# Strided 512-byte block loads for an fp32 conditional MLP kernel: every fourth unit in a tile, one transfer for two W slices, and a reordered expert turn

## The chip, the core and the metric

The kernel runs on one core of a Trainium2 chip. The metric is device time in microseconds of one execution: 1680.95 us for the kernel before, the median of 3 runs (1678.97 to 1681.01).

## What is computed

```python
# x (64, 128, 512) fp32; cat_ids (64,) in 0..63; exp_ids (64,) in 0..15
x = x + (einsum('bsd,bdh->bsh', x, W[cat_ids]) + b[cat_ids][:, None, :])            # L0, W (64, 512, 512)
h = gelu(einsum('bnd,hd->bnh', x, fc1_w) + fc1_b)                                     # fc1_w (2048, 512), exact gelu
shared = einsum('bnh,sh->bns', h, fc2_w) + fc2_b                                      # fc2_w (384, 2048)
expert = einsum('bnh,bph->bnp', h, experts_w[exp_ids]) + experts_b[exp_ids][:, None, :]  # experts_w (16, 128, 2048)
x = x + concat([shared, expert], -1)
```

Each of the 64 batches picks its own L0 matrix (1 MB) and its own expert (1 MB).

## The kernel before, in words

**Tiling.** 16 groups of GB = 4 batches. The 2048 hidden units are cut into NC = 16 tiles of 128, one per step c. In step c TensorE does `fc1(g, c)` (12 matmuls of 128x512: 4 slices of D, each as three fp32r products of high and low parts), `fc2(g, c-1)` (12 matmuls, 3 for each of 4 batches; 384 shared columns and 128 of the expert) and, in the eight steps of `L0_STEPS`, two slices (6 matmuls) of the L0 product of the next group. All weights and activations are split into a high part (ACT casts) and a low part (VectorE subtracts, all at the helper's L599).

**Layouts.** TensorE contracts over the partitions, so x, y (the result of L0), h and the experts must be transposed. The shared weights and the first group's x and y are transposed by TensorE (`turn`, L745), in the first group only. In all later groups it is done by DMA and VectorE: a DMA brings 32x32 blocks to their place (x: L341, y by way of a DRAM copy: L524, experts: L386), where each contiguous piece in DRAM is r = 32 floats, 128 bytes, and `nc.vector.transpose` turns all blocks of a 128x512 tile (x L614, y L627, experts L643). Hidden tile c of the kernel is rows `hidden_rows(c)*128 ...` of fc1_w; a quad of four steps shares one load of expert blocks (`load_experts`, 4 batches x 4 DMAs of 64 KB).

**Order.** Every engine runs an order written out by hand. VectorE in step c: low parts of W slices (`w_low`) and of x (`x_low`) if the step has L0 slices, `copy_last` (L661), `e_low`, at c = 0 the four results of the previous group (L680), then `turn_next_e` (the turn of expert tile c+1, L643) before `h_high` (L668) and `h_low` for c > 0 (after `h_low` for c = 0), then `turn_x` at c = 0 and at the end of a batch's L0 slices, `turn_y` two steps after them, `y_sum` (L634); after step 15 four `y_low`. In the first group `prep_low` of one shared weight tile stands between `h_high` and `h_low` and one at the end of the step. ACT: `w_high`, `x_high`, `e_high`, y DMAs, gelu (L544), `prep_high` with the next prep DMA. SP issues all other DMAs in order: in `load_l0_in(g+1, c)` first x blocks, then W slices (two 256 KB transfers into two slots, `w_in[0]`, `w_in[1]`, each behind the `w_lo` of its slot's last user), then the L0 bias and x; then at c = 0 the stores of the previous group, then the expert blocks of batch (c+1)%4. GpSimd adds biases (L463, L473, L474).

**Who waits for whom.** `fc2(g, c)` waits for `h_lo`, `e_lo` and `last_ready` of tile c; an L0 slice waits for `w_lo` and `x_lo`; `fc1(g+1, 0)` waits for all four `y_lo`. `turn_e` of a quad's first tile waits for 16 DMAs.

Of the kernel before, what the change touches and what calls it, by code (L numbers as in the profile page):

```python
# [25 lines left out]
ACT = mybir.ActivationFunctionType  # L26
P = 128
# [3 lines left out]
def build(nc, x, cat_ids, exp_ids, l0_w, l0_b, fc1_w, fc1_b, fc2_w, fc2_b, exp_w, exp_b, out):  # L31
# [17 lines left out]
    L0_STEPS = (1, 3, 5, 7, 9, 10, 11, 12)  # L49
# [5 lines left out]
    with ctx:  # L55
# [41 lines left out]
        b1_rows = x_raw[0:NC, 0:P]  # L97
# [20 lines left out]
        w_in = [sem(f"w_in{i}") for i in range(WSLOTS)]  # L118
# [17 lines left out]
        b1_turned = sem("b1_turned")  # L136
# [8 lines left out]
        b1_ready = sem("b1_ready")  # L145
# [79 lines left out]
        def hidden_rows(c):  # L225

            return (c % QUAD) * (NC // QUAD) + c // QUAD
# [81 lines left out]
        def load_prep(eng, t):  # L309
# [3 lines left out]
            dst = prep_tile(t) if PREP[t][0] == "fc1" else prep_tile(t).rearrange("p (k h) -> p k h", k=QUAD)  # L313
            eng.dma_start(dst, prep_src(t)).then_inc(prep_in[prep_slot(t)], 16)
# [3 lines left out]
        def _(sp):  # L318
# [12 lines left out]
            def load_x_blocks(G, b):  # L331
# [12 lines left out]
            def load_w(G, j, cat):  # L344

                if first(G):
                    after(sp, w_lo, j - W0SLOTS + 1)
                else:
                    after(sp, w_lo, G * NC + j - WSLOTS + 1)
                k = j % KD  # L350
                sp.dma_start(w_slot(G, j), l0_w[bass.ds(cat, 1), k * P:(k + 1) * P, :].rearrange("o d n -> (o d) n"))\  # L351
                  .then_inc(w0_in[j % W0SLOTS] if first(G) else w_in[j % WSLOTS], 16)
# [516 lines left out]
```

## Time and profile before

| | us |
|---|---|
| time, median of 3 runs | 1680.95 (1678.97 to 1681.01) |
| the profiled execution's own time | 1681.4 |
| its span, first to last instruction | 1679.6 |
| TensorE busy / VectorE busy / ACT busy / GpSimd busy | 1639.4 / 1176.4 / 551.9 / 195.1 |
| mean granted TensorE clock | 0.997 |

A granted clock of 1.00 is the 2.4 GHz level, 0.5 the 1.2 GHz level. Matmuls are pipelined, so the time that one costs is read from the distance between starts of blocks, not from its own duration. The idle time in brackets in a row is the engine's idle time before the row, with what released it. SPq and ACTq are the issuing of DMAs.

### The profile page before, as it was taken

The page shows a single profiled execution, that of the slowest core. Times are in us where ns is not written, and L with a number is a line of the kernel's source. Part 1 is how long each engine was busy: PE and PEld are TensorE (multiplying, and loading weights), DVE is VectorE, ACT ScalarE, POOL GpSimd, SP SyncE. Part 2 cuts the span into 40 slices and gives each one's busy share as a digit, 9 for nine tenths or more (in the row PEclk, how much of TensorE's full clock was granted, in tenths as well). Part 3 has the DMA queues.
Part 4 walks back from the last instruction along what each step waited for, and adds up shares of the span by engine and source line. Part 5 has one row for each costly group of instructions (what it writes and reads, how often), then busy time and mean ns, then how long its engine had stood idle before and what let it go on. Part 6 is the DMA issues. An engine that isn't in the chain of part 4 may idle for free.

```text
span 1679.6 us, 28015 instructions
## 1 busy us (share of the span) xinstructions
PE 1639.4 (98%) x7065; PEld 1315.8 (78%) x7065; DVE 1176.4 (70%) x2004; ACT 551.9 (33%) x927; POOL 195.1 (12%) x195
## 2 busy tenths in 40 slices
PE   7899999999999999999999999999999999999999
PEld 5778887877878778787877878778787787878887
DVE  5677667776777767776776677767777677767754
ACT  4343333333323333333332333333333333333321
POOL 0200100111020010200102001110200102001110
PEclk9999999999999999999999999999999999999999
DMA  7886776757677575775767767686775757757630
GB/s 207 185 190 150 147 149 147 156 129 162 127 163 151 131 156 118 167 159 133 149 133 160 156 144 157 131 157 135 163 153 131 155 118 164 163 131 151 134 61 26
DMA packets 884826, 243.44 MB, mean 145 GB/s; under 512 B 803688, under 2 KB 818168, under 8 KB 884732
## 3 DMA queue, kind: packets, MB, share of 16 engines
q1 hardware_dynamic: 740732, 203.75, 57.1%
q10 hardware_dynamic: 144000, 38.82, 10.7%
q14 instruction: 82, 0.67, 0.1%
q8 instruction: 12, 0.20, 0.1%
HBM read 209.93 MB, written 32.51 MB: 144 GB/s over the span
## 4 chain that ended last, share of the span: by engine, by line
PE 66%; SPq 20%; issue 8%; DMA 3%; DVE 2%; ACT 1%; DVEq 0%
PE ps_out L814 30%; PE ps_h L799 14%; PE ps_e L799 13%; PE ps_y L786 8%; SPq L386 8%; SPq L341 4%; SPq L320 2%; DMA e_blocks<-in_L_cond_experts_w 2%; SPq L399 2%; SPq L351 1%; SPq L393 1%; PE ps_t L745 1%; DVE e_whole L643 1%; DVE h L599 1%; DVE w2e L599 1%
## 5 line engine op out<-in xcount | busy, mean ns | idle before, releaser
L814 PE MATMUL ps_out<-w2e,h 128*128 128x512 f32 x3072 | 758.0, 396 | 10.0 <-DVE h L599 10.0
L814 PEld LDWEIGHTS ps_out<-w2e,h 128*128 128x128 f32 x3072 | 574.3, 188 | 152.5 <-DVE h L599 15.9
L799 PE MATMUL ps_e<-y_t,w 128*128 128x512 f32 x1536 | 376.8, 395 | 1.4 <-DVE y_t L599 1.4
L799 PE MATMUL ps_h<-y_t,w 128*128 128x512 f32 x1536 | 375.7, 394 | 0.0
L799 PEld LDWEIGHTS ps_e<-y_t,w 128*128 128x128 f32 x1536 | 290.7, 189 | 66.9 <-DVE y_t L599 1.6
L799 PEld LDWEIGHTS ps_h<-y_t,w 128*128 128x128 f32 x1536 | 288.5, 188 | 65.7
L643 DVE STREAM_TRANSPOSE e_whole<-e_blocks 128x512 f32<-128x512 f32 x256 | 182.0, 711 | 109.3 <-DMA e_blocks<-in_L_cond_experts_w 100.9
L530 ACT CAST w2e<-e_whole 128x512 fp32r<-128x512 f32 x256 | 158.6, 620 | 284.4 <-PE ps_out L814 157.4
L463 POOL TENSOR_TENSOR x_raw<-x_raw,b_all 128x512 f32<-128x512 f32 x60 | 85.3, 1422 | 1354.9 <-DMA x_raw<-in_x 1303.2
L499 ACT CAST w_split<-w_raw 128x512 fp32r<-128x512 f32 x244 | 145.7, 619 | 243.7 <-DMA w_raw<-in_L_cond_W 174.4
L599 DVE TENSOR_TENSOR w_split<-w_raw,w_split 128x512 fp32r<-128x512 f32 x244 | 161.1, 688 | 84.6 <-ACT w_split L499 83.7
L668 DVE CAST h<-g_raw 128x512 fp32r<-128x512 f32 x256 | 120.8, 472 | 125.4 <-ACT g_raw L544 124.0
L786 PE MATMUL ps_y<-w_split,x_t 128*128 128x512 f32 x732 | 193.1, 399 | 12.0 <-DVE x_t L599 9.6
L544 ACT ACTIVATE g_raw<-ps_e,b 128x512 f32<-128x512 f32 x128 | 88.1, 688 | 344.9 <-PE ps_e L799 302.3
L599 DVE TENSOR_TENSOR w2e<-e_whole,w2e 128x512 fp32r<-128x512 f32 x256 | 191.7, 749 | 9.9 <-ACT w2e L530 9.8
L599 DVE TENSOR_TENSOR h<-g_raw,h 128x512 fp32r<-128x512 f32 x256 | 192.7, 753 | 8.4
L786 PEld LDWEIGHTS ps_y<-w_split,x_t 128*128 128x128 f32 x732 | 137.2, 190 | 49.9 <-DVE w_split L599 14.8
L544 ACT ACTIVATE g_raw<-ps_h,b 128x512 f32<-128x512 f32 x128 | 87.8, 686 | 198.9 <-PE ps_h L799 188.8
L661 DVE CAST w2e<-w2e 128x512 fp32r<-128x512 f32 x256 | 115.2, 450 | 25.6 <-PE ps_out L814 25.4
L473 POOL TENSOR_TENSOR resid<-y,b_all 128x384 f32<-128x384 f32 x64 | 73.3, 1145 | 49.4 <-DMA out<-resid 49.1
L627 DVE STREAM_TRANSPOSE w_raw<-x_blocks 128x512 f32<-128x512 f32 x30 | 21.3, 711 | 67.7 <-DMA x_blocks<-y_rows 67.7
L614 DVE STREAM_TRANSPOSE x_whole_t<-x_blocks 128x512 f32<-128x512 f32 x60 | 41.9, 699 | 15.7 <-DMA x_blocks<-in_x 15.6
(71 smaller groups left out, 431.3 us busy)
## 6 DMA issues: line engine op xcount, KB each, us to landing
e_blocks<-in_L_cond_experts_w SPq DMA_DIRECT2D x1024, 64.0 KB, 2.9
w_raw<-in_L_cond_W SPq DMA_DIRECT2D x248, 256.0 KB, 2.9
out<-resid SPq DMA_DIRECT2D x64, 256.0 KB, 4.7
x_blocks<-in_x SPq DMA_DIRECT2D x240, 64.0 KB, 2.4
b_all<-in_L_cond_b SPq DMA_DIRECT2D x60, 256.0 KB, 4.3
x_raw<-in_x SPq DMA_DIRECT2D x60, 256.0 KB, 4.6
y_rows<-y ACTq DMA_DIRECT2D x60, 256.0 KB, 2.8
x_blocks<-y_rows ACTq DMA_DIRECT2D x240, 64.0 KB, 3.7
```

The lines of the kernel that those rows point to most:

```text
L386: sp.dma_start(e_blocks[i * Q:(i + 1) * Q, quad % 2, b, :] .rearrange("q (c j r) -> q c j r", c=QUAD, r=Q), src).then_inc(e_in[quad % 2], 16)
L463: nc.gpsimd.tensor_tensor(x_raw[:, :], x_raw[:, :], b0_all[:, :], ALU.add).then_inc(xb_ready, 1)
L499: nc.scalar.copy(split_slot(G, j)[:, 0, :], w_slot(G, j)).then_inc(w_hi, 1)
L530: nc.scalar.copy(experts_of(c % 2, 0), e_whole[:, :].rearrange("p (q v n) -> p q v n", q=GB // 2, v=2))\
L544: nc.scalar.activation(g_raw[:, c % 2, :], h_bank(c)[:, :], ACT.Gelu, bias=b1[:, hidden_rows(c):hidden_rows(c) + 1])\
L599: return nc.vector.tensor_tensor(dst, whole, high.bitcast(F32), ALU.subtract)
L643: nc.vector.transpose(e_whole[:, :], e_blocks[:, (c // QUAD) % 2, :, off:off + P]).then_inc(e_turned, 1)
L661: nc.vector.tensor_copy(ring[:, c % 2, :, :, 1, :], w2[:, :, c, SHARED - P:].unsqueeze(2).to_broadcast([P, 2, GB // 2, P]))\
L668: nc.vector.tensor_copy(h[:, c % 2, 0, :], g_raw[:, c % 2, :]).then_inc(h_hi, 1)
L786: last = nc.tensor.matmul(l0_bank(G, b)[:, :], x_halves(G, b)[:, a, k, :], split_slot(G, j)[:, w, :], start=(k == 0 and n == 0), stop=(k = ...
L799: last = nc.tensor.matmul(h_bank(c)[:, :], w1[:, w, k, c * P:(c + 1) * P], y_t[:, a, k, :, :].rearrange("p b s -> p (b s)"), start=(k == 0 ...
L814: last = nc.tensor.matmul(ps_out[b][:, :], h[:, c % 2, a, b * S:(b + 1) * S], fc2_columns(c, c % 2, w, b), start=(c == 0 and n == 0), stop ...
```

## The change

The data that share a tile are chosen differently: instead of 128 consecutive units of D or of the hidden dimension, a tile takes every fourth (D: unit 4p+k in slice k; hidden: unit u*512 + 4p + c in tile c of quad u). Then one 128-float (512-byte) piece in DRAM holds the blocks of four tiles, and the DMAs of x, y and expert blocks move 512-byte pieces where they moved 128-byte ones. The picking moves into the reads of the transposes: VectorE's `turn_x`, `turn_y`, `turn_e` and TensorE's `turn` read with a step of 4 floats (16 bytes) and write contiguously as before. fc1_b is loaded straight into its place (TensorE transpose, ACT copy and the semaphores `b1_turned`, `b1_ready` go); fc2_w tiles load as 2 KB rows. The two W slices of a pair are neighbouring rows and come in one 512 KB transfer, one semaphore, behind the `w_lo` of both slots. `turn_next_e` stands behind `h_low` in every step. The first L0 step moves from 1 to 2 and `turn_x(g+1, 0)` from step 0 to step 1. On SP the x blocks come after W, L0 bias and x; the second x block load moves from step 1 to step 2; the stores come after the step's expert blocks; in the first group fc2_b and the expert biases move from step 0 to step 1. On TensorE the prep turn of step 0 comes before `fc1`.

```diff
-    L0_STEPS = (1, 3, 5, 7, 9, 10, 11, 12)
+    L0_STEPS = (2, 3, 5, 7, 9, 10, 11, 12)
-        w_in = [sem(f"w_in{i}") for i in range(WSLOTS)]
+        w_in = sem("w_in")
+        def every_fourth(whole, k):
+            return whole.rearrange("p (m k) -> p k m", k=KD)[:, k]
         def prep_src(t):
             if PREP[t][0] == "fc1":
-                m = hidden_rows(PREP[t][1])
-                return fc1_w[m * P:(m + 1) * P, :]
+                m = PREP[t][1]
+                return fc1_w.rearrange("(u p c) d -> u c p d", u=NC // QUAD, c=QUAD)[m // QUAD, m % QUAD]
             _, n, q = PREP[t]
-            return fc2_w[n * P:(n + 1) * P, :].rearrange("p (k u h) -> u p k h", k=QUAD, h=P)[q]
+            return fc2_w[n * P:(n + 1) * P, q * QUAD * P:(q + 1) * QUAD * P]
...
-                    src = x[bass.ds(G * GB + b, 1), :, :].rearrange("o (j q) (k i r) -> i q k (o j) r", q=Q, k=KD, r=Q)[i]
-                    sp.dma_start(x_blocks[i * Q:(i + 1) * Q, :].rearrange("q (k j r) -> q k j r", k=KD, r=Q), src)\
+                    src = x[bass.ds(G * GB + b, 1), :, :].rearrange("o (j q) (i n) -> i q (o j) n", q=Q, n=P)[i]
+                    sp.dma_start(x_blocks[i * Q:(i + 1) * Q, :].rearrange("q (j n) -> q j n", n=P), src)\
...
+            def load_w_pair(G, p, cat):
+                after(sp, w_lo, G * NC + 2 * p)
+                src = l0_w[bass.ds(cat, 1), :, :].rearrange("o (p h k) n -> h (o p) (k n)", h=KD // 2, k=2)[p % 2]
+                sp.dma_start(w_raw[:, 0:WSLOTS, :].rearrange("p k n -> p (k n)"), src).then_inc(w_in, 16)
...
             def load_l0_in(G, c):
-                for b, step in ((0, 0), (1, 1), (2, L0_STEPS[1] + 3), (3, L0_STEPS[3] + 3)):
-                    if c == step:
-                        load_x_blocks(G, b)
                 for p in range(2 * GB):
                     if c == (0 if p == 0 else L0_STEPS[p - 1]):
                         if p % 2 == 0:
                             load_l0_in.cat = category(G, p // 2)
-                        load_w(G, 2 * p, load_l0_in.cat)
-                        load_w(G, 2 * p + 1, load_l0_in.cat)
+                        load_w_pair(G, p, load_l0_in.cat)
                 for b in range(GB):
                     if c == (0 if b == 0 else L0_STEPS[2 * b - 1] + 1):
                         load_b0(G, b, load_l0_in.cat)
                         load_x(G, b)
+                for b, step in ((0, 0), (1, L0_STEPS[0]), (2, L0_STEPS[1] + 3), (3, L0_STEPS[3] + 3)):
+                    if c == step:
+                        load_x_blocks(G, b)
...
-                            .rearrange("o (j q) (c u i r) -> u i q c (o j) r", q=Q, c=QUAD, i=P // Q, r=Q)[quad, i]
+                            .rearrange("o (j q) (u i n) -> u i q (o j) n", q=Q, i=P // Q, n=P)[quad, i]
...
-                    if c == 0 and not first(g):
-                        store(g - 1)
                     b, quad = (c + 1) % GB, (c + 1) // QUAD + 1
                     if quad < NC // QUAD:
                         load_experts(g, quad, idx, [b])
...
+                    if c == 0 and not first(g):
+                        store(g - 1)
...
+            def split_of(whole_t):
+                return whole_t.rearrange("p (k j q) -> p k j q", k=KD, q=Q)
+            def blocks_of(blocks):
+                return blocks.rearrange("p (j r k) -> p k j r", k=KD, r=Q)
...
-                nc.vector.transpose(x_whole_t[:, :], x_blocks[:, :]).then_inc(x_turned, 1)
+                nc.vector.transpose(split_of(x_whole_t[:, :]), blocks_of(x_blocks[:, :])).then_inc(x_turned, 1)
...
-                off = (c % QUAD) * P
-                nc.vector.transpose(e_whole[:, :], e_blocks[:, (c // QUAD) % 2, :, off:off + P]).then_inc(e_turned, 1)
+                src = e_blocks[:, (c // QUAD) % 2, :, :].rearrange("p b (j r c) -> p c (b j) r", c=QUAD, r=Q)[:, c % QUAD]
+                nc.vector.transpose(e_whole[:, :].rearrange("p (a q) -> p a q", q=Q), src).then_inc(e_turned, 1)
...
-                    if c > 0:
-                        turn_next_e(g, c, more)
                     h_high(g, c)
                     prep_low(prep_in_step(g, c, 0))
                     h_low(g, c)
-                    if c == 0:
-                        turn_next_e(g, c, more)
+                    turn_next_e(g, c, more)
                     prep_low(prep_in_step(g, c, 1))
                     if more:
-                        if c == 0:
+                        if c == L0_STEPS[0] - 1:
                             turn_x(g + 1, 0)
...
+                    if c == 0:
+                        turn_prep(prep_in_step(g, c, 0))
                     fc1(g, c)
-                    turn_prep(prep_in_step(g, c, 0))
+                    if c > 0:
+                        turn_prep(prep_in_step(g, c, 0))
```

## Rows read from the trace of the kernel before

**Rows 1.** The page: engines' busy time with share and instructions; DMA packets.

```profile
PE 1639.4 (98%) x7065; PEld 1315.8 (78%) x7065; DVE 1176.4 (70%) x2004; ACT 551.9 (33%) x927; POOL 195.1 (12%) x195
DMA packets 884826, 243.44 MB, mean 145 GB/s; under 512 B 803688, under 2 KB 818168, under 8 KB 884732
```

**Rows 2.** Timeline of TensorE (start, length, what): group starts, plain steps, L0 steps.

```profile
158.88 2.96 PE L799 MATMUL ps_e<-y_t,w 128*128 128x512 f32 x12
...
832.31 2.91 PE L799 MATMUL ps_e<-y_t,w 128*128 128x512 f32 x12
...
839.23 2.91 PE L799 MATMUL ps_h<-y_t,w 128*128 128x512 f32 x12
...
1586.81 2.96 PE L799 MATMUL ps_e<-y_t,w 128*128 128x512 f32 x12
...
1606.36 2.93 PE L799 MATMUL ps_e<-y_t,w 128*128 128x512 f32 x12
...
1617.52 2.93 PE L799 MATMUL ps_e<-y_t,w 128*128 128x512 f32 x12
```

**Rows 3.** Waits of TensorE, whole span: total us, times, longest.

```profile
PE ps_out L814 <- DVE h L599: 10.0, 13, 1.2
PE ps_y L786 <- DVE x_t L599: 9.6, 12, 1.6
```

**Rows 4.** Timeline of TensorE in the eighth group, the two gaps.

```profile
878.19 2.96 PE L814 MATMUL ps_out<-w2e,h 128*128 128x512 f32 x12
881.62 1.65 PE L786 MATMUL ps_y<-w_split,x_t 128*128 128x512 f32 x6 [0.47 <-DVE x_t L599]
...
895.59 2.91 PE L799 MATMUL ps_e<-y_t,w 128*128 128x512 f32 x12
899.26 3.06 PE L814 MATMUL ps_out<-w2e,h 128*128 128x512 f32 x12 [0.76 <-DVE h L599]
```

**Rows 5.** Timeline of VectorE in the same group.

```profile
870.79 0.68 DVE L599 TENSOR_TENSOR y_t<-ps_t,y_t 128x512 fp32r<-128x512 f32 x1
...
879.60 1.29 DVE L599 TENSOR_TENSOR w_split<-w_raw,w_split 128x512 fp32r<-128x512 f32 x2 [0.91 <-ACT w_split L499]
...
897.46 0.71 DVE L643 STREAM_TRANSPOSE e_whole<-e_blocks 128x512 f32<-128x512 f32 x1 [3.76 <-DMA e_blocks<-in_L_cond_experts_w]
```

**Rows 6.** Timeline of SP's queue in the same group.

```profile
872.34 2.95 SPq L341 DMA_DIRECT2D x_blocks<-in_x  x4
876.20 0.88 SPq L351 DMA_DIRECT2D w_raw<-in_L_cond_W  x2
...
889.10 6.46 SPq L386 DMA_DIRECT2D e_blocks<-in_L_cond_experts_w  x8
```

**Rows 7.** Timeline of TensorE in the first group.

```profile
62.13 3.04 PE L814 MATMUL ps_out<-w2e,h 128*128 128x512 f32 x12
68.58 1.09 PE L745 MATMUL ps_t<-ident,prep_raw 128*128 128x128 f32 x4 [3.40 <-issue]
69.32 2.91 PE L786 MATMUL ps_y<-w_split,x_t 128*128 128x512 f32 x6
...
75.81 0.60 PE L745 MATMUL ps_t<-ident,prep_raw 128*128 128x128 f32 x4
```

**Rows 8.** Timeline of VectorE in the first group, the same place.

```profile
66.86 0.71 DVE L643 STREAM_TRANSPOSE e_whole<-e_blocks 128x512 f32<-128x512 f32 x1 [2.55 <-DMA e_blocks<-in_L_cond_experts_w]
```

**Rows 9.** Stretches: us, busy us (instructions) by engine, granted clock, DMA share, GB/s.

```profile
60.00:80.00 20.00, 16.60 (x70) 13.27 (x69) 11.40 (x18) 5.10 (x10) 3.48 (x4) 0.83 0.74 167
...
825.37:853.09 27.72, 27.72 (x122) 22.51 (x120) 18.47 (x33) 9.70 (x16) 3.25 (x2) 1.00 0.80 163
```

**Rows 10.** Groups of instructions: busy us, mean ns of one, idle before them.

```profile
L643 DVE STREAM_TRANSPOSE e_whole<-e_blocks 128x512 f32<-128x512 f32 x256 | 182.0, 711 | 109.3 <-DMA e_blocks<-in_L_cond_experts_w 100.9
...
L680 DVE TENSOR_TENSOR resid<-ps_out,resid 128x512 f32<-128x512 f32 x32 | 21.7, 677 | 0.0
L680 DVE TENSOR_TENSOR resid<-ps_out,resid 128x128 f32<-128x128 f32 x64 | 15.2, 278 | 0.0
```

**Rows 11.** Issues from SP: ns of one, min/median/max, first and last start.

```profile
L386 SPq DMA_DIRECT2D e_blocks<-in_L_cond_experts_w x1024: 582/582/1673, 21.3 to 1631.5; - x171
...
L351 SPq DMA_DIRECT2D e_blocks<-in_L_cond_W x8: 331/333/344, 9.6 to 20.8; - x8
```

More of the change, by code:

```diff
@@ L312, in load_prep @@
             after(eng, prep_turned, max(prep_earlier(t), default=-1) + 1)
-            dst = prep_tile(t) if PREP[t][0] == "fc1" else prep_tile(t).rearrange("p (k h) -> p k h", k=QUAD)
-            eng.dma_start(dst, prep_src(t)).then_inc(prep_in[prep_slot(t)], 16)
+            eng.dma_start(prep_tile(t), prep_src(t)).then_inc(prep_in[prep_slot(t)], 16)
         @block.sync
@@ L339, in load_x_blocks, with load_first_w @@
                 for i in range(P // Q):
-                    src = x[bass.ds(G * GB + b, 1), :, :].rearrange("o (j q) (k i r) -> i q k (o j) r", q=Q, k=KD, r=Q)[i]
-                    sp.dma_start(x_blocks[i * Q:(i + 1) * Q, :].rearrange("q (k j r) -> q k j r", k=KD, r=Q), src)\
+                    src = x[bass.ds(G * GB + b, 1), :, :].rearrange("o (j q) (i n) -> i q (o j) n", q=Q, n=P)[i]
+                    sp.dma_start(x_blocks[i * Q:(i + 1) * Q, :].rearrange("q (j n) -> q j n", n=P), src)\
                       .then_inc(x_blocks_in, 16)
[L344 to L352, printed above, removed]
+            def load_first_w(j, cat):
+                after(sp, w_lo, j - W0SLOTS + 1)
+                src = l0_w[bass.ds(cat, 1), :, :].rearrange("o (p k) n -> k (o p) n", k=KD)[j % KD]
+                sp.dma_start(w_slot(0, j), src).then_inc(w0_in[j % W0SLOTS], 16)
+            def load_w_pair(G, p, cat):
+                after(sp, w_lo, G * NC + 2 * p)
+                src = l0_w[bass.ds(cat, 1), :, :].rearrange("o (p h k) n -> h (o p) (k n)", h=KD // 2, k=2)[p % 2]
+                sp.dma_start(w_raw[:, 0:WSLOTS, :].rearrange("p k n -> p (k n)"), src).then_inc(w_in, 16)
             def load_b0(G, b, cat):
@@ L384, in load_experts @@
                         src = exp_w[bass.ds(idx[b], 1), :, :]\
-                            .rearrange("o (j q) (c u i r) -> u i q c (o j) r", q=Q, c=QUAD, i=P // Q, r=Q)[quad, i]
-                        sp.dma_start(e_blocks[i * Q:(i + 1) * Q, quad % 2, b, :]
-                                     .rearrange("q (c j r) -> q c j r", c=QUAD, r=Q), src).then_inc(e_in[quad % 2], 16)
+                            .rearrange("o (j q) (u i n) -> u i q (o j) n", q=Q, i=P // Q, n=P)[quad, i]
+                        sp.dma_start(e_blocks[i * Q:(i + 1) * Q, quad % 2, b, :].rearrange("q (j n) -> q j n", n=P), src)\
+                          .then_inc(e_in[quad % 2], 16)
             def load_expert_bias(g, idx):
@@ L408, in _ @@
                     cat = category(0, j // KD)
-                load_w(0, j, cat)
+                load_first_w(j, cat)
                 if j % KD == 0:
@@ L438, in body @@
                         load_experts(g + 1, quad - NC // QUAD, next_idx, [b])
-                    if first(g) and c == 0:
+                    if c == 0 and not first(g):
+                        store(g - 1)
+                    if first(g) and c == 1:
                         sp.dma_start(b2_all[:, :], fc2_b.rearrange("(o n) -> o n", o=1).to_broadcast([P, SHARED]))\
@@ L496, in w_high @@
                 else:
-                    after(act, w_in[j % WSLOTS], 16 * ((G - 1) * (NC // WSLOTS) + j // WSLOTS + 1))
+                    after(act, w_in, 16 * ((G - 1) * (NC // WSLOTS) + j // WSLOTS + 1))
                 after(act, l0_done, j - S0SLOTS + 1 if first(G) else G * NC + j - 1)
@@ L543, in gelu @@
                 after(act, h_lo, g * NC + c - 1)
-                nc.scalar.activation(g_raw[:, c % 2, :], h_bank(c)[:, :], ACT.Gelu, bias=b1[:, hidden_rows(c):hidden_rows(c) + 1])\
+                nc.scalar.activation(g_raw[:, c % 2, :], h_bank(c)[:, :], ACT.Gelu, bias=b1[:, c:c + 1])\
                     .then_inc(gelu_done, 1)
@@ L751, in turn_x @@
                 after(pe, x_lo, b)
-                turn(ps_t, [resid[:, b, k * P:(k + 1) * P] for k in range(KD)]).then_inc(x_turned, 1)
+                turn(ps_t, [every_fourth(resid[:, b, :], k) for k in range(KD)]).then_inc(x_turned, 1)
             def turn_y(b):
                 pe.wait_ge(y_ready, b + 1)
-                if b == 0:
-                    pe.wait_ge(b1_ready, 1)
                 after(pe, y_lo, b)
-                turn(y_bank(b), [y[:, b, k * P:(k + 1) * P] for k in range(KD)])\
+                turn(y_bank(b), [every_fourth(y[:, b, :], k) for k in range(KD)])\
                     .then_inc(y_turned, 1)
@@ L771, in turn_prep @@
                     pe.wait_ge(x_lo, GB)
-                turn(prep_bank(t), [prep_tile(t)[:, n * P:(n + 1) * P] for n in range(4)]).then_inc(prep_turned, 1)
+                turn(prep_bank(t), [every_fourth(prep_tile(t), k) for k in range(KD)]).then_inc(prep_turned, 1)
             def l0_slice(G, j):
```

22 lines of the change are left out of this document (6 added, 16 removed).

## The prediction

> **What bounds the kernel now.** First the page: TensorE is busy 1639.4 of 1679.6 us [rows 1], so nearly everything that can be won is in its gaps, unless its own work changes. It doesn't in the steady groups: the same 432 matmuls of 512 columns with the same shapes. Then TensorE's timeline, for what a group would take without gaps [rows 2]: two plain steps take 1617.52 - 1606.36 = 11.16, so 5.58 each; a step with L0 slices takes 839.23 - 832.31 = 6.92. Eight of each are 8 x 5.58 + 8 x 6.92 = 100.0 us. The 14 groups from 158.88 to 1586.81 took 1427.9, or 102.0 each. So 2.0 us in each group, 27.9 us in all, are gaps. The waits name them [rows 3]: fc2 waits for h 13 times (10.0 us) and the first L0 slice for x_t 12 times (9.6 us). In the timeline of one group [rows 4] they cost more than the idle time in brackets: fc2 that starts at 878.19 is through 2.8 later, at 880.99, and the slice starts at 881.62, 0.63 late; fc1 from 895.59 is through at 898.38, fc2 starts at 899.26, 0.88 late; and the restarts are 0.1 us longer each. That is 1.7 of the 2.0.
>
> **Why they wait.** The h gap: VectorE, which runs in order, stood 3.76 us at the turn of the expert tile, waiting for its blocks, with h_high and h_low queued behind it [rows 5]. Those blocks were issued late, eight transfers from 889.10 to 895.6 [rows 6], since SP issues 64 KB in 0.58 us and pays some 0.14 more between two (2.95 for four). The x_t gap: SP issues the x blocks at 872.34 and W only at 876.20 [rows 6]; W lands, is cast, and VectorE starts its low parts at 879.60 after a wait [rows 5]; x_t comes after them.
>
> The first group has the largest single gap: fc2 from 62.13 is through at 65.0, the next prep turn starts at 68.58 [rows 7]. VectorE stood 2.55 us at the expert turn [rows 8], and the prep's low part, for which the turn waits, is queued behind it. Then TensorE ran at the lower clock: the stretch from 60 to 80 us shows a granted 0.83 [rows 9], and from 68.58 to 75.81 it did 4 transposes, 6 and 12 matmuls, 7.2 us for what takes 0.36 + 1.38 + 2.8 = 4.5 at full speed. Gap and clock: 3.5 + 2.7 = 6.2 us.
>
> **The change, part by part.**
>
> *Turn behind h.* Removes the expert blocks' wait from ahead of h and of prep_low. The 0.9 us gap goes in the groups that show it. What is late next is the end of the group: the turn of step 15 now stands between h_low and the four y_low. Before, the last y_low began at 870.79 and ended near 871.5 [rows 5]; fc1 of the next group could start at 872.6, so there is 1.1 us of room. The turn takes 0.71 [rows 10] as it is: it fits. At 1.24 (below) it doesn't: 0.1 to 0.3 us of waiting for y_t and 0.1 for the restart, per group.
>
> *First L0 step 1 to 2, W ahead of x blocks.* W is issued some 3 us earlier and used a step (5.58 us) later; turn_x moves along by one step. The 0.6 us gap goes. New deadlines: turn_x(0) runs at the end of VectorE's step 1, w_low and x_low at the start of step 2, the slice after fc1 and fc2 of step 2, and that leaves 0.7 us even with slow turns. Also the step 2 load of the second pair waits for both low parts of step 2; SP's queue behind it holds the second x blocks and the quad's last expert blocks; these are used in step 3 after h_low, over 2 us later than they land. In step 10 the fourth x blocks, formerly issued ahead of W, now stand behind the wait for step 10's w_low, about 4 us later, and turn_x(3) and y_sum are queued on VectorE for them, with x_low(3) for step 11 behind. I find the margin before the slice of step 11 to be 0.6 to 1 us with slow turns. I set 0.2 us per group for it, between 0 and 1.
>
> *512-byte pieces.* 803,688 of 884,826 packets are under 512 bytes [rows 1]; nearly all become a quarter as many. This removes no TensorE time by itself; it shortens landings and so supports the two items above. Issue time per 64 KB lies between 0.33 (the simplest W load) and 0.58 (as now) [rows 11]; at either SP keeps up, and SP is off the path once the two waits are gone. The Trainium skill (DMA: Bandwidth & Descriptors, Specifications) puts the line-rate minimum at 512 bytes and says that smaller pieces are read, modified and written; it agrees with the direction and adds no term.
>
> *One 512 KB transfer for a pair.* It replaces two issues (0.88 us for two [rows 6]) by one, and waits for both slots instead of one: up to 0.7 us later for the first slice, 0 for the second. The two casts are consecutive on ACT, so nothing starts before the second low part of the pair before. Cost 0 to 0.7 us in the three back-to-back steps 10 to 12; hidden by the 5.6 us of fc1 and fc2 that come ahead of the slices.
>
> *Turns that read every fourth float.* The trace has no such read. 376 turns (256 experts, 60 x, 60 y) take 711 ns [rows 10]. Lower bound: no change, 0.71. Upper: an element costs (677 - 278) / 384 = 1.04 ns [rows 10], so if each of 512 took one more such beat, 0.71 + 0.53 = 1.24 us. I take 1.24, the unfavourable end, because each read goes to another 16 bytes, which no row excludes from costing. VectorE would be busy 376 x 0.53 = 199 us more, 1376, still under TensorE. Locally: in four L0 steps in a row VectorE is busy 18.47 of 27.72 us [rows 9]; with 7 turns in them that is 22.2, 80%. So the heaviest stretch fits, with less room for its waits. The Trainium skill speaks against this part: SBUF — State Buffer (Door 1: The DMA port swizzle) has 16-byte lines, full speed wants two hits on a line, and each access that crosses to a new one pays a penalty. By that rule the turns are slow, by the lower bound they are free; it gives no figure for VectorE, and no run here shows it yet.
>
> *TensorE's turns with the same step.* 23 tiles in the first group at 0.36 us, between 0 and +0.36 each if doubled: 0 to 8.3 us. I take 2: part of it falls into gaps that are there anyway.
>
> *First group, rest.* 6.2 us of gap and clock go. A wait of 1.4 us for a prep load goes with the lighter DMA traffic. VectorE has two prep low parts more per step, and slow turns make L0 steps there about as long as TensorE's: +1.5 (0 to 4). The prep turn ahead of fc1(0) and the direct b1 load: 0, they lie in idle time. Together -6.2 - 1.4 + 2 + 1.5 = -4.1.
>
> **The sum.** Steady groups: 27.9 less what stays, 0.3 (y_t) + 0.2 (x_low in step 11) = 0.5 x 14 = 7.0, so -20.9. First group -4.1. Total -25.0: span 1679.6 - 25.0 = 1654.6. The profiled execution took 1.8 more than its span (1681.4) and is 0.45 above the median: 1654.6 + 1.8 - 0.4 = 1656.0.
>
> **The rivals.**
>
> *Turns as fast as before* (0.71). Nothing is left at y_t and in step 11 but 0.1 per group: -26.5; first group -7.6 + 1 = -6.6. Total -33.1, 1648. For it: nothing in the trace says that a stride costs. Chance 0.25.
>
> *In-order VectorE returns half the gain.* Slow turns and the DMA waits that remain (x and y blocks) add up so that some L0 step a group waits again for w_split or x_t, and the first group shows more prep gaps: 1.0 us more per group, 14, plus 3: 1673. For it: 80% busy in order with four partners. Against: fc2 needs h_low only 5.6 to 7 us after fc1's end. Chance 0.16.
>
> *Slower: VectorE becomes the bound.* One mechanism: a strided turn costs two more beats, 0.71 + 1.07 = 1.78. Per group VectorE's other work is (1176.4 - 376 x 0.71) / 16 = 56.8; with 24 turns of 1.78 it is 99.5, and with some 5 us of waits that can't be filled 104.5 against 102.0 now: 14 x 2.5 = 35, 1716. It decides from t = (102 - 5 - 56.8) / 24 = 1.68 us per turn. Chance 0.12.
>
> *The gains are only exchanged*: the gap at x_t becomes one at y_t or x_low of the same size, or the loads don't come earlier because SP's wait moved instead. 1680. Chance 0.05.
>
> **How the numbers follow.** Forecast 0.42 (1656, own range 1648 to 1666), fast turns 0.25, half returned 0.16, exchanged 0.05, slower 0.12. A measurement of this kernel can tell about 0.2%, 3.4 us. Faster 0.42 + 0.25 + 0.16 = 0.83, of which I give 0.02 to slower for a turn only just over the threshold: 0.81; same 0.05; slower 0.14. The range 1645 to 1678 holds the first three cases, about 0.8.
>
> **What would show it.** The mean of L643 (0.71, 1.24 or more) decides between the cases. Right: waits of fc2 for h and of L0 for x_t gone from the steady groups, group period near 100.5, L643's wait for DMA small, packets near 300,000, and no gap near 65 us with full clock after it. Wrong: a wait for y_t at each group start over 0.5 us, TensorE waiting for w_split or x_t in steps 10 to 12, VectorE over 85% busy, or TensorE's L745 blocks in the first group clearly longer than 0.36 us.

## The result and the profile after

| | before | after |
|---|---|---|
| median, us | 1680.98 (4 runs, 1678.97 to 1682.89) | 1657.82 (4 runs, 1655.17 to 1659.78) |
| ratio, 95% interval | | 0.9859 [0.9843, 0.9876] |
| span of the profiled execution | 1679.6 | 1656.5 |

The change is 1.4% faster, 23.1 us by the two spans. The page of the kernel after, as [rows 1]:

```profile
PE 1635.6 (99%) x7064; PEld 1320.3 (80%) x7064; DVE 1317.6 (80%) x2004; ACT 550.3 (33%) x926; POOL 219.2 (13%) x195
DMA packets 285898, 243.43 MB, mean 147 GB/s; under 512 B 32232, under 2 KB 233064, under 8 KB 285804
```

TensorE's busy time hardly moves (1639.4 to 1635.6), VectorE has 141 us more, the packets are a third. The waits of TensorE from 160 to 1600 us, the steady groups, as [rows 3] (in the kernel before that stretch holds all of them). One line is left:

```profile
PE ps_y L784 <- DVE x_t L602: 2.0, 2, 1.5
```

TensorE's timeline: the starts of the second and of the last group, the ninth group's start, and the place of the first L0 slices, now in step 2, as [rows 2, 4]. Counted in this way, the group of [rows 4 to 6] is the ninth as well; it starts at 872.6.

```profile
157.84 3.03 PE L797 MATMUL ps_e<-y_t,w 128*128 128x512 f32 x12
...
854.89 5.76 PE L812 MATMUL ps_out<-w2e,h 128*128 128x512 f32 x24
860.49 3.02 PE L797 MATMUL ps_e<-y_t,w 128*128 128x512 f32 x12
...
871.69 2.96 PE L812 MATMUL ps_out<-w2e,h 128*128 128x512 f32 x12
874.77 1.64 PE L784 MATMUL ps_y<-w_split,x_t 128*128 128x512 f32 x6
...
1563.72 2.95 PE L797 MATMUL ps_e<-y_t,w 128*128 128x512 f32 x12
```

(1563.72 - 157.84) / 14 = 100.4 us per group, against 102.0; six of the 14 groups take 100.14 and one 100.16, which is what the gapless sum of 100.0 meant. Of this group's 0.28 us at the slices (871.69 + 2.80 = 874.49) the reason is on VectorE, timeline of the same group:

```profile
859.68 0.68 DVE L602 TENSOR_TENSOR y_t<-ps_t,y_t 128x512 fp32r<-128x512 f32 x1
...
868.86 1.10 DVE L646 STREAM_TRANSPOSE e_whole<-e_blocks 128x512 f32<-128x512 f32 x1
871.76 1.10 DVE L617 STREAM_TRANSPOSE x_whole_t<-x_blocks 128x512 f32<-128x512 f32 x1 [1.79 <-DMA x_blocks<-in_x]
872.78 1.25 DVE L602 TENSOR_TENSOR w_split<-w_raw,w_split 128x512 fp32r<-128x512 f32 x2
```

The turns, mean ns of one, as [rows 10]; and the stretch of four L0 steps, as [rows 9]:

```profile
L646 DVE STREAM_TRANSPOSE e_whole<-e_blocks 128x512 f32<-128x512 f32 x256 | 279.2, 1091 | 0.0
```

```profile
825.75:853.70 27.95, 27.95 (x122) 22.73 (x121) 21.15 (x33) 8.67 (x14) 1.65 (x1) 1.00 0.43 126
```

A turn takes 1.09 us, its wait for expert blocks (100.9 us before) is zero, VectorE is busy 21.15 of 27.95 us, 76%. Last, SP's issues, as [rows 11], and TensorE's start: first turn, start of the first group's fc1, and the place of [rows 7].

```profile
L383 SPq DMA_DIRECT2D e_blocks<-in_L_cond_experts_w x1024: 316/317/1860, 22.1 to 1608.3; - x171
```

```profile
5.13 1.10 PE L745 MATMUL ps_out<-ident,prep_raw 128*128 128x128 f32 x4 [5.13 <-DMA prep_raw<-in_L_cond_fc_w]
...
40.00 4.60 PE L797 MATMUL ps_e<-y_t,w 128*128 128x512 f32 x12 [0.92 <-DVE y_t L602]
46.63 0.95 PE L745 MATMUL ps_t<-ident,prep_raw 128*128 128x128 f32 x4 [2.02 <-issue]
...
66.60 3.04 PE L812 MATMUL ps_out<-w2e,h 128*128 128x512 f32 x12
69.48 0.64 PE L745 MATMUL ps_t<-ident,prep_raw 128*128 128x128 f32 x4
```

So the 23.1 us are: ahead of the first fc1 40.00 against 36.03, +4.0; first group 157.84 - 40.00 = 117.8 against 122.85, -5.0; 14 groups 1405.9 against 1427.9, -22.0; the last group and the end are equal to 0.1 us.

### The profile page after: what moved, and what is told of

It reads as the page before. It is cut to its first block, busy times and chain, and to the rows that moved or that the text cites. A ratio compares the mean times of both kernels' runs of the same rounds, so it can differ in the third digit from the quotient of the medians.

```text
span 1656.5 us, 27539 instructions
## 1 busy us (share of the span) xinstructions
PE 1635.6 (99%) x7064; PEld 1320.3 (80%) x7064; DVE 1317.6 (80%) x2004; ACT 550.3 (33%) x926; POOL 219.2 (13%) x195
## 3 DMA queue, kind: packets, MB, share of 16 engines
q1 hardware_dynamic: 238572, 203.74, 45.1%
## 4 chain that ended last, share of the span: by engine, by line
PE 95%; issue 1%; SPq 1%; DVE 1%; DMA 1%; ACT 0%; DVEq 0%
PE ps_out L812 41%; PE ps_e L797 21%; PE ps_h L797 21%; PE ps_y L784 11%; PE ps_t L745 1%; DMA x_blocks<-in_x 0%; PE ps_h L784 0%; SPq L316 0%; DMA prep_raw<-in_L_cond_fc_w 0%; DVE w_split L602 0%; SPq L383 0%; PE ps_out L745 0%; SPq L390 0%; SPq L337 0%; PE ps_e L745 0%
## 5 line engine op out<-in xcount | busy, mean ns | idle before, releaser
L646 DVE STREAM_TRANSPOSE e_whole<-e_blocks 128x512 f32<-128x512 f32 x256 | 279.2, 1091 | 0.0
L671 DVE CAST h<-g_raw 128x512 fp32r<-128x512 f32 x256 | 124.6, 487 | 172.7 <-ACT g_raw L542 172.5
L461 POOL TENSOR_TENSOR x_raw<-x_raw,b_all 128x512 f32<-128x512 f32 x60 | 91.4, 1524 | 1281.5 <-DMA x_raw<-in_x 1235.1
L497 ACT CAST w_split<-w_raw 128x512 fp32r<-128x512 f32 x244 | 141.0, 618 | 232.8 <-DMA w_raw<-in_L_cond_W 183.3
L602 DVE TENSOR_TENSOR w_split<-w_raw,w_split 128x512 fp32r<-128x512 f32 x244 | 168.3, 729 | 51.5 <-ACT w_split L497 51.5
L602 DVE TENSOR_TENSOR w2e<-e_whole,w2e 128x512 fp32r<-128x512 f32 x256 | 184.3, 720 | 18.0 <-ACT w2e L528 17.9
L784 PEld LDWEIGHTS ps_y<-w_split,x_t 128*128 128x128 f32 x732 | 136.9, 189 | 39.6 <-DVE w_split L602 3.6
L664 DVE CAST w2e<-w2e 128x512 fp32r<-128x512 f32 x256 | 128.7, 503 | 0.0
L617 DVE STREAM_TRANSPOSE x_whole_t<-x_blocks 128x512 f32<-128x512 f32 x60 | 64.7, 1079 | 47.2 <-DMA x_blocks<-in_x 47.2
L471 POOL TENSOR_TENSOR resid<-y,b_all 128x384 f32<-128x384 f32 x64 | 83.0, 1297 | 75.8 <-DMA out<-resid 74.9
L503 ACT CAST x_t<-x_whole_t 128x512 fp32r<-128x512 f32 x60 | 37.3, 622 | 58.2 <-DVE x_whole_t L617 58.2
```

The source lines that it names most:

```text
L461: nc.gpsimd.tensor_tensor(x_raw[:, :], x_raw[:, :], b0_all[:, :], ALU.add).then_inc(xb_ready, 1)
L471: nc.gpsimd.tensor_tensor(resid[:, b, 0:SHARED], y[:, b, 0:SHARED], b2_all[:, :], ALU.add)
L497: nc.scalar.copy(split_slot(G, j)[:, 0, :], w_slot(G, j)).then_inc(w_hi, 1)
L602: return nc.vector.tensor_tensor(dst, whole, high.bitcast(F32), ALU.subtract)
L646: nc.vector.transpose(e_whole[:, :].rearrange("p (a q) -> p a q", q=Q), src).then_inc(e_turned, 1)
L664: nc.vector.tensor_copy(ring[:, c % 2, :, :, 1, :], w2[:, :, c, SHARED - P:].unsqueeze(2).to_broadcast([P, 2, GB // 2, P]))\
```

## The experiments

Theories at the start: the new order removes the two waits and the larger pieces support it (the prediction's); against it, the order alone has the gain, or the layout alone has it. "Steady" below is TensorE's mean group period over 14 groups, read from its timeline as above (before 102.0, after 100.4). Each ratio is to the kernel before, measured beside the variant (its medians there are 1682.24 to 1682.64 us), so a variant is compared with the change (0.9859) by its ratio.

**Order alone.** The kernel before with the following, and with the change's other moves: x blocks behind W in SP's queue, stores behind the experts, turn_x(0) in step 1, the prep turn of step 0 ahead of fc1, fc2_b and the expert biases in step 1 of the first group.

```diff
-    L0_STEPS = (1, 3, 5, 7, 9, 10, 11, 12)
+    L0_STEPS = (2, 3, 5, 7, 9, 10, 11, 12)
-                    if c > 0:
-                        turn_next_e(g, c, more)
                     h_high(g, c)
                     prep_low(prep_in_step(g, c, 0))
                     h_low(g, c)
-                    if c == 0:
-                        turn_next_e(g, c, more)
+                    turn_next_e(g, c, more)
```

> The kernel before with the new order alone: turn behind h, L0 steps 2, 3, 5, ..., x blocks behind W, stores behind experts, prep turn of step 0 ahead of fc1; layout, 128-byte pieces, packed reads of the turns (0.71 us) and two 256 KB W transfers as before. Theory (the order removes the two waits, the layout only supports it): group period near 100.5, 1655 to 1660. If the order is all of the gain, this is faster than the changed kernel, since its turns are 0.38 us shorter: 1650 to 1656. Rival (SP's issuing at 0.58 us a piece is the cause): expert and x blocks still land late, the waits only move to x_t or y_t: 1665 to 1680.

Measured: 1680.52 us, ratio 0.9987 [0.9975, 0.9999], steady 102.0. At most 0.25% is gained, against 1.4%. The waits of TensorE in the steady groups:

```profile
PE ps_y L783 <- DVE x_t L599: 9.0, 15, 1.5
PE ps_y L783 <- DVE w_split L599: 8.2, 13, 1.2
PE ps_out L811 <- DVE h L599: 0.6, 1, 0.6
```

The wait for h is nearly gone, the wait for x_t stays although its step is later, and one for w_split has come, in each of 13 groups at the slices of step 3. SP's timeline in the ninth group (start 873.67), its first W pair, the x blocks and the second W pair:

```profile
877.49 0.88 SPq L351 DMA_DIRECT2D w_raw<-in_L_cond_W  x2
879.50 2.97 SPq L341 DMA_DIRECT2D x_blocks<-in_x  x4
892.06 1.01 SPq L351 DMA_DIRECT2D w_raw<-in_L_cond_W  x2
```

The same in the kernel after (start 860.49):

```profile
864.24 0.34 SPq L350 DMA_DIRECT2D w_raw<-in_L_cond_W  x1
865.72 1.90 SPq L337 DMA_DIRECT2D x_blocks<-in_x  x4
874.46 0.35 SPq L350 DMA_DIRECT2D w_raw<-in_L_cond_W  x1
```

SP issues without a pause from the first pair to the second in both, and it takes 14.6 us against 10.2. The second pair, due one step after the first now, comes 18.4 us into the group against 14.0: that is the wait for w_split. The x blocks are all issued 8.8 us into the group against 7.1. The transfers themselves take no longer with the order alone (median from issue to landing: x blocks 2.7 us against 3.6, W 2.9 against 4.4, expert blocks 2.8 against 2.6). So at these two places it is SP's issue time, and not the landing of small pieces, that takes the gain of the order away.

**Layout alone.** The changed kernel with the old order everywhere, so these lines and the x blocks, the stores and the prep turn at their old places:

```diff
-    L0_STEPS = (2, 3, 5, 7, 9, 10, 11, 12)
+    L0_STEPS = (1, 3, 5, 7, 9, 10, 11, 12)
...
+                    if c > 0:
+                        turn_next_e(g, c, more)
...
-                    turn_next_e(g, c, more)
+                    if c == 0:
+                        turn_next_e(g, c, more)
```

> The changed kernel with the order of the kernel before: turn ahead of h for c > 0, first L0 step 1, x blocks ahead of W, stores ahead of experts, prep turn of step 0 behind fc1; new are the 512-byte pieces, the strided turns and the one 512 KB W transfer. Theory (the order has most of the gain): the x_t wait of step 1 stays or grows by the longer turn_x, the h wait shrinks since blocks land earlier: 1664 to 1678. Rival (the layout alone has the gain): 1655 to 1660. If the strided turns hurt where they stand ahead of h: above 1681.

Measured: 1691.84 us, 1.0065 [1.0043, 1.0087], steady 102.5: slower, above the ranges of the theory and the rival. The third case, strided turns that hurt ahead of h, doesn't show in the wait for h. Waits in the steady groups:

```profile
PE ps_y L787 <- DVE x_t L602: 23.5, 14, 4.0
PE ps_out L815 <- DVE h L602: 0.3, 1, 0.3
```

Here too the wait for h is gone, with the turn ahead of h. The x_t wait is 2.4 times as large; in the ninth group it went from 0.5 to 1.0 us. What it hangs on is W. ACT's first cast of W in the ninth group, before (start 872.6) and then here (start 876.37):

```profile
878.94 1.18 ACT L499 CAST w_split<-w_raw 128x512 fp32r<-128x512 f32 x2 [2.66 <-DMA w_raw<-in_L_cond_W]
```

```profile
883.27 1.14 ACT L497 CAST w_split<-w_raw 128x512 fp32r<-128x512 f32 x2 [3.22 <-DMA w_raw<-in_L_cond_W]
```

SP issued W 1.1 us sooner in the group than before (2.5 against 3.6), but the cast starts 6.9 us into it against 6.3, because the one transfer of 512 KB lands in 4.4 us where the first of two of 256 KB took 2.7; the low parts of W and of x follow it. turn_x waits for no DMA here (5.8 us into the group in every one, against 5.4). So with the step at 1 the merged transfer costs time; whether layout alone with two transfers would gain was not run. Neither half has the gain.

**Turn ahead of h again,** in the changed kernel:

```diff
+                    if c > 0:
+                        turn_next_e(g, c, more)
                     h_high(g, c)
                     prep_low(prep_in_step(g, c, 0))
                     h_low(g, c)
-                    turn_next_e(g, c, more)
+                    if c == 0:
+                        turn_next_e(g, c, more)
```

> The changed kernel with one part undone: the expert turn stands in front of h_high again for c > 0. Theory (the turn had to go behind h because it is now 1.09 us long and its blocks can be late): fc2 waits for h again, though less than before since the blocks now land early; the turn of 1.09 us itself lies ahead of h, where gelu leaves some room. Expected 1657 to 1668, waits of fc2 for h 0 to 10 us. Rival (the lighter DMA traffic alone cured the wait for blocks, the position of the turn is worth nothing): 1655 to 1659, no wait of fc2 for h in the steady groups; the four y_low at the group's end even come a little earlier.

Measured: 1660.31 us, 0.9863 [0.9845, 0.9882], steady 100.3, waits of fc2 for h 0.3 us in all. In the steady groups the turn's place is worth nothing, as the rival had it, though the median is 1.3 us above the rival's range. The first group took 122.0 us instead of 117.8, with four waits of 0.2 to 2.4 us ahead of prep turns (5.8 us in all, against 3.4). The ratios are 0.0004 apart (0.7 us): that the place helps the first group rests on one profile of each.

**First L0 step back at 1,** in the changed kernel (`L0_STEPS = (1, 3, ...)`, with which turn_x(0) goes to step 0 and the second x blocks to step 1).

> The changed kernel with the first L0 step back at 1 (turn_x of batch 0 at step 0, its x blocks issued at step 0 as before, the second ones at step 1). Theory (the first L0 step had to move, since SP's part at the group's start and the longer turn_x don't fit ahead of step 1): the wait of the first L0 slice for x_t or w_split comes back with 1 to 2 us per group, 1672 to 1690. In the run with the whole old order it was 23.5 us. Rival (the x_t wait of that run came from x blocks ahead of W and the stores, not from the step): 1657 to 1663.

Measured: 1757.1 us, 1.044 [1.0423, 1.0458], steady 107.5, far outside both expectations. Two rows, the waits of TensorE and of VectorE over the whole span:

```profile
PE ps_y L784 <- DVE x_t L602: 74.1, 14, 6.7
```

```profile
DVE x_whole_t L617 <- DMA x_blocks<-in_x: 98.4, 29, 6.4
```

The x blocks, issued after W, L0 bias and x, come up to 6.4 us late for a turn in step 0, and TensorE waits 5.3 us a group. The rest of the 7.1 us lost per group goes with the clock: mean granted 0.975, and in 13 of the 14 groups, those with waits of 4.9 to 6.7 us, a stretch at the 1.2 GHz level of 3.4 or 6.8 us. The group with a wait of 1.7 us has none. With x blocks ahead of W (layout alone) the same step cost 23.5 us of waiting. So moving the step is the part without which the rest loses. The x blocks behind W need the moved step; the moved step doesn't need them there (the run with x blocks ahead of W, below).

**W slices as two transfers,** in the changed kernel:

```diff
-                sp.dma_start(w_raw[:, 0:WSLOTS, :].rearrange("p k n -> p (k n)"), src).then_inc(w_in, 16)
+                for i in range(2):
+                    src = l0_w[bass.ds(cat, 1), :, :].rearrange("o (p k) n -> k (o p) n", k=KD)[(2 * p + i) % KD]
+                    sp.dma_start(w_raw[:, i, :], src).then_inc(w_in, 16)
```

> The changed kernel with the pair's two W slices as two 256 KB transfers of single rows again, both issued behind the same wait and counted by the same semaphore. It undoes the merging alone. Theory (the merging is worth one SP issue of 0.35 us and nothing on the path, because SP now waits for others some 590 us in all): 1656 to 1660. Rival (4 KB pieces land faster, and the steps 10 to 12 need that): waits for w_split in these steps, 1662 to 1672.

Measured: 1657.24 us, 0.9859 [0.9838, 0.9881], steady 100.4. With the step at 2 the merging is worth nothing that can be told.

**Packed reads in VectorE's turns,** in the changed kernel, all three turns in the form that they had before the change. It leaves out the picking of every fourth unit, so it computes other numbers and only its time is of use:

```diff
-                nc.vector.transpose(split_of(x_whole_t[:, :]), blocks_of(x_blocks[:, :])).then_inc(x_turned, 1)
+                nc.vector.transpose(x_whole_t[:, :], x_blocks[:, :]).then_inc(x_turned, 1)
```

> The changed kernel with VectorE's three kinds of turns reading packed floats instead of every fourth; it leaves out the picking of units, so the numbers that it computes are other ones. It prices the strided read in place. Turns 0.71 us instead of 1.09. Theory (VectorE has the room, 80% busy): the 141 us of extra VectorE time cost TensorE almost nothing, 1653 to 1658, what is left is the wait for x blocks in step 1. Rival (the longer turns are what makes the remaining 0.4 us per group and the first group's gap at step 3 or 5): 1646 to 1651.

Measured: 1654.86 us, 0.983 [0.981, 0.9851], turns 703 ns, steady 100.3. In place, 141 us of extra VectorE time cost some 3 us by the medians and 5 by the ratios, and the intervals of the two kernels overlap.

**Issues doubled,** in the changed kernel, for expert and x blocks:

```diff
-                        sp.dma_start(e_blocks[i * Q:(i + 1) * Q, quad % 2, b, :].rearrange("q (j n) -> q j n", n=P), src)\
-                          .then_inc(e_in[quad % 2], 16)
+                        for a in (0, Q // 2):
+                            sp.dma_start(e_blocks[i * Q + a:i * Q + a + Q // 2, quad % 2, b, :].rearrange("q (j n) -> q j n", n=P), src[a:a + Q // 2])\
+                              .then_inc(e_in[quad % 2], 16)
```

> The changed kernel with SP's expert and x block transfers cut in two (16 partitions each, pieces still 512 bytes), so that SP issues twice as many, 0.317 us each: 0.63 a pair against the 0.58 that one 64 KB transfer of 128-byte pieces took before. It takes the issue time back and keeps the piece size. Theory (SP's issue time was the binding side of the small pieces; with the new order alone SP couldn't keep up and the gain was nil): the waits for x_t and w_split at the first L0 slices come back, group period 101 to 102, 1668 to 1682. Rival (the transfers' own time, 68% against 54% busy DMA engines, was the binding side): 1656 to 1661.

Measured: 1776.12 us, 1.0564 [1.054, 1.0588], steady 108.3. This doubles the issue time, where the expectation had reckoned 0.63 us for two issues: it left out the time between them. SP's timeline, four issues of the kernel after, and then eight of this one:

```profile
877.07 1.82 SPq L383 DMA_DIRECT2D e_blocks<-in_L_cond_experts_w  x4
```

```profile
934.91 3.82 SPq L385 DMA_DIRECT2D e_blocks<-in_L_cond_experts_w  x8
```

From start to start, the four issues of [rows 6] took (2.95 - 0.58) / 3 = 0.79 us; after the change it is (1.82 - 0.32) / 3 = 0.50, and doubled (3.82 - 0.32) / 7 = 0.50 for half the bytes. So 64 KB cost SP 0.79, 0.50 and 1.00 us, and the 80 of a group 63, 40 and 80. SP's waits, whole span, the largest of each kernel, doubled issues and after:

```profile
SPq L398 <- DVE resid L685: 35.4, 4, 34.5
SPq L351 <- DVE w_split L604: 26.5, 32, 3.2
SPq L385 <- DVE e_whole L648: 12.4, 12, 3.2
```

```profile
SPq L350 <- DVE w_split L602: 256.7, 79, 11.6
SPq L383 <- DVE e_whole L646: 163.3, 17, 12.3
```

SP's waits add up to 82 us with doubled issues, 600 after, 191 before and 202 with the order alone. The pages say the same in their section 4, the chain of work that ended last. Before, after, order alone, doubled issues:

```profile
PE 66%; SPq 20%; issue 8%; DMA 3%; DVE 2%; ACT 1%; DVEq 0%
```

```profile
PE 95%; issue 1%; SPq 1%; DVE 1%; DMA 1%; ACT 0%; DVEq 0%
```

```profile
PE 62%; SPq 17%; issue 8%; DMA 5%; DVE 3%; ACTq 3%; ACT 1%; DVEq 0%
```

```profile
PE 40%; SPq 32%; issue 15%; DMA 6%; DVE 5%; ACT 2%; ACTq 1%; DVEq 0%
```

With doubled issues a third of the chain is SP's issuing, though the DMA engines are less busy (queue 1: 39.9% against 45.1%), the pieces are still 512 bytes, and the transfers land no later after their issue (median 2.0 us for expert blocks against 2.6, 2.2 for x blocks against 3.6). TensorE waits at the same two places as with the order alone: for x_t in step 2 in 13 of the 14 groups, for w_split in step 3 in all of them. That SP's issuing can bound this kernel is shown. The size is not that of the kernel before (1.00 us against 0.79), and part of the loss is the clock (mean granted 0.979), so this run doesn't price the 0.79 us.

**x blocks of batch 0 ahead of W,** in the changed kernel, ahead of the load of W in SP's queue:

```diff
+                if c == 0:
+                    load_x_blocks(G, 0)
...
-                for b, step in ((0, 0), (1, L0_STEPS[0]), (2, L0_STEPS[1] + 3), (3, L0_STEPS[3] + 3)):
+                for b, step in ((1, L0_STEPS[0]), (2, L0_STEPS[1] + 3), (3, L0_STEPS[3] + 3)):
```

> The changed kernel with one edit forward: at step 0 the x blocks of batch 0 are issued ahead of W, L0 bias and x (all later ones stay behind W). Theory (the 0.3 us per group that stay at the first L0 slice are VectorE's wait of 1.8 us for these x blocks in step 1, which SP issues last): group period 100.1 instead of 100.4, 1653 to 1656. Rival (W then lands later and w_low is late instead): 1657 to 1662.

Measured: 1659.77 us, 0.9872 [0.9845, 0.9898], steady 100.6. In the steady groups there are now two waits for w_split (2.7 us) and one for x_t (1.2), where the kernel after has two for x_t (2.0). The rival held: the wait is exchanged, and the place of these x blocks is worth nothing that can be told.

**Prep turn of step 0 behind fc1,** in the changed kernel:

```diff
-                    if c == 0:
-                        turn_prep(prep_in_step(g, c, 0))
...
-                    if c > 0:
-                        turn_prep(prep_in_step(g, c, 0))
+                    turn_prep(prep_in_step(g, c, 0))
```

> The changed kernel with TensorE's prep turn of step 0 behind fc1 again, as before. In the changed kernel's trace TensorE stands 2.0 us ahead of the next prep turn and then runs 3.4 us at the 1.2 GHz level; in the trace of before the gap there was 1.6 us and the clock stayed up. Theory (the moved turn leaves the gap unfilled and the clock falls): 1654 to 1657, no half clock around 47 to 50 us. Rival (the turn was in idle time either way and the clock's fall comes from elsewhere): 1657 to 1660, the same half-clock stretches.

Measured: 1657.98 us, 0.9859 [0.9837, 0.9881], steady 100.5. The stretch at 1.2 GHz around 47 us was absent in this profile and one around 40 stayed; the time is the same. Which of the early stretches show varies between profiles of nearly equal kernels, so this is not settled and it isn't worth a measurable time.

**Expert ids read later.** SP's reads of the ids behind the step 0 loads:

```diff
-                idx = first_experts if first(g) else [index(exps, g * GB + b, exp_w.shape[0]) for b in range(GB)]
                 for c in range(NC):
                     if more:
                         load_l0_in(g + 1, c)
+                    if c == 0:
+                        idx = first_experts if first(g) else [index(exps, g * GB + b, exp_w.shape[0]) for b in range(GB)]
```

In the changed kernel:

> The changed kernel with one edit forward: SP's four reads of the group's expert ids stand behind the loads for the next group's L0 at step 0 instead of ahead of them. In the trace SP issues nothing for 7.7 us around each group's start. Theory (that pause is mostly these reads, and it makes the x blocks of batch 0 late for turn_x, the last wait that stays in the steady groups): SP's first load comes some 4 us earlier, the period is 100.1, 1651 to 1655. Rival (the pause is the loop's branch or a wait that is met late): no change, 1656 to 1660.

Measured: 1656.77 us, 0.9851 [0.9834, 0.9867], steady 100.4. SP's timeline here and in the kernel after, its first load of the ninth group:

```profile
854.92 1.92 SPq L390 DMA_DIRECT2D be_all<-in_L_cond_experts_b  x4
862.19 0.34 SPq L350 DMA_DIRECT2D w_raw<-in_L_cond_W  x1
```

```profile
854.57 1.92 SPq L390 DMA_DIRECT2D be_all<-in_L_cond_experts_b  x4
864.24 0.34 SPq L350 DMA_DIRECT2D w_raw<-in_L_cond_W  x1
```

The pause shrinks from 7.7 to 5.3 us, so the four reads were 2.4 us of it and not most of it. The time doesn't change by anything that can be told.

With the first L0 step at 1 as well:

> The same with the first L0 step back at 1, the edit that alone made the changed kernel 1757 us. Theory (there the L0 part was late because SP's pause and its queue came ahead of turn_x in step 0, with everything of VectorE behind it): with SP 4 us earlier most of the 7 us per group come back, but not all, since the slices are due 5.6 us earlier: 1660 to 1700. Rival (the longer turns are what doesn't fit in steps 0 and 1): 1740 to 1757 as without the edit.

Measured: 1711.54 us, 1.0174 [1.0152, 1.0197], wait for x_t 41.9 us instead of 74.1, steady 104.3, between the two expectations. 2.4 us of SP per group are worth 45.6 us of time here, the clock's share in it: SP's late start in the group is a large part of what makes step 1 too early.

In the kernel before, as its only edit:

> The kernel before with that one edit: the reads of the expert ids behind the step 0 loads. No other part of the change. Theory (the x_t wait of the kernel before was SP's late start, too): the 9.6 us of waiting for x_t shrink to under 3, the h wait stays or shrinks a little since SP gets to the expert blocks earlier: 1664 to 1674. Rival (SP's issuing is full anyway, the reads only move the pause behind the W loads): 1677 to 1682.

Measured: 1673.23 us, 0.9953 [0.9938, 0.9969], steady 101.3. Waits in the steady groups:

```profile
PE ps_out L814 <- DVE h L599: 9.0, 7, 2.1
PE ps_y L786 <- DVE x_t L599: 3.3, 6, 0.5
```

The x_t wait falls from 9.6 to 3.3 us, so SP's late start made two thirds of it in the kernel before; the wait for h stays. By the ratios this edit is worth a third of the whole change. No variant beats the changed kernel by more than the runs scatter.

Undone one at a time in the changed kernel, the turn's place, the merged transfer, the place of the first x blocks and that of the prep turn are each worth nothing that can be told. What is left is the layout and the first L0 step at 2, with the places of the stores and of the later x blocks, which no run changed by themselves. A kernel with the layout and the moved step alone was not run.

## Why the prediction was right

The forecast was 1656.0, the measured time 1657.8. By its steps:

- **Bound and ideal group:** right. 100.0 forecast, 100.14 to 100.16 in half of the groups, and TensorE's work unchanged.
- **Steady groups:** -20.9 forecast, -22.0 measured. The sum is right, but how it comes about was told wrongly in four places, so that it came out this near is partly luck.
  - *Turn behind h* was given the 0.9 us gap. With the turn ahead of h and the new layout the wait is 0.3 us in all, and with the turn behind h and the old layout it is 0.6. Either cures it.
  - *"At either [0.33 or 0.58 us] SP keeps up, and SP is off the path"* is the step that failed. With the new order and 0.58 us issues the gain was nil. The layout was costed as a helper worth no TensorE time that shortens landings, and it is the condition of all of it, by SP's issues (0.79 to 0.50 us for 64 KB). The prediction had some 0.14 us between two issues; its own row, 2.95 us for four, gives (2.95 - 4 x 0.58) / 3 = 0.21. And it passed over the 20% of SPq in the chain of the page before.
  - *"W is issued some 3 us earlier"* didn't happen. W went out 3.6 us into the group before (876.20 - 872.6) and 3.75 after (864.24 - 860.49; medians of 14 groups 3.6 and 3.5), since SP comes to the group's start later; the x blocks, formerly 0.3 us ahead of it, are issued 5.2 us into it. The room at the first slices is that of the moved step alone. The rival "exchanged" had named this ("SP's wait moved instead") with a chance of 0.05.
  - *What stays:* 0.3 us at y_t was charged and nothing shows (fc2 from 854.89 is through at 860.49, when fc1 starts; the last y_low began 0.8 ahead of that), nor does the 0.2 in step 11. The room of the 1.24 us turn wasn't needed at 1.09. What is left, 0.4 us per group on average, shows at the first L0 slices (two waits of 2.0 us in all, and the 0.28 of the ninth group), where the prediction had 0.7 us of margin: VectorE waits 1 to 3 us for the x blocks there, which SP issues last.
- **Turns:** 0.71 to 1.24, taken at 1.24; measured 1.09, +0.38 us or 0.74 ns per element where one more beat of 1.04 was assumed. VectorE had +141 us instead of +199. The fast-turn case would have had 1648; taking the strides out gave 1654.9, so it put too high a price on them. The rule of the Trainium skill (SBUF — State Buffer, Door 1: The DMA port swizzle) that each new 16-byte line costs something agrees with the trace, 703 ns packed against 1091 strided.
- **TensorE's turns:** +2 taken in 0 to 8.3. A tile takes 0.39 us for 0.36, so 23 x 0.03 = 0.7 us.
- **First group:** -4.1 forecast, -5.0 measured from the first fc1 on. The gap and the half clock near 65 us are gone (69.48 follows on 66.60), and a gap of 2.0 us with 3.4 us at the 1.2 GHz level has come near 47.
- **Ahead of the first fc1:** costed at 0, measured +4.0. This is the term missed; the 0.9 and 1.1 us won elsewhere beyond the forecast hide half of it, and the span is 1.9 us above the forecast. The first prep turn starts at 5.13 instead of 3.67 us. In the three profiles with contiguous rows it waited 3.5 to 3.7 us, in the eleven of kernels with every fourth row (after and experiments) 4.3 to 5.1; so the first loads land later by about 1 us. A gap of 2.0 us follows at 18.09, where the kernel before had 0.2, and from 19 to 24 us the granted clock is 0.66, where before it was 1.00. It belongs to the layout: fc1 starts at 39.6 us with layout alone and at 36.8 with order alone. VectorE's strided reads aren't it (39.2 with packed turns). Whether it is the rows 8 KB apart, fc1_b in 16-byte pieces or TensorE's strided turns was not tried; it stays open.
- **The slower rival** (turns of 1.68 us or more) was off by 0.6 us in t. But there was another way to be slower that wasn't seen: with the layout, the order or the moved step left out, or SP's issues doubled, the kernel takes 1680.5, 1691.8, 1757.1 and 1776.1 us.

## What to carry to other kernels

When an in-order DMA-issuing queue feeds an in-order chain, count its time from start to start of its issues, over a whole period, and not only the landing time of one: here 80 issues at 0.79 us against 0.50 decided whether the reordering paid. The share of the issuing queue in the chain of the page, 20% here, says beforehand that it isn't off the path. Test the halves of a change that has a layout half and an order half: each alone gave nothing or a loss (1680.5 and 1691.8), both together -1.4%. And look at what the queue does at the loop's boundary: moving four register reads behind the first loads was worth 0.5% of the kernel before.

## What the runs showed of the hardware

A VectorE transpose of 128x512 fp32 that reads with a step of 16 bytes took 1.09 us against 0.70 to 0.71 packed; TensorE's weight load of a 128x128 fp32 tile for a transpose took 209 ns (median) against 140. A 64 KB load from SP took 0.58 us to issue in 128-byte pieces and 0.32 in 512-byte ones, and a load of half the bytes also took 0.32. One 512 KB transfer landed in 4.4 us (median), 256 KB of the same in 2.9 before; for the changed kernel they were worth the same, and with the first L0 step at 1 the later landing of the larger one lengthened the wait. The clock followed the gaps: with one wait of 4.9 to 6.7 us per group there was a stretch of 3.4 or 6.8 us at the 1.2 GHz level in each of 13 groups; in the steady groups of the kernel before, with waits of up to 1.6 us, there was none.
